# A decayed running sum by shifted additions on VectorE in place of products on TensorE

## The reference, cut to what matters

```
h      = rmsnorm(layernorm(x)) * g_res @ W_in.T + b_in
u      = rmsnorm(ctx)[:, :512] * g_init * exp(-0.001)
s[p]   = a * s[p-1] + u[p]            # the scan: a = 1 - exp(-0.001), about 0.001
x      = x + h + s[plug]
y      = layernorm(x); y_prev = y one row earlier
r      = sigmoid((mu_r*y + (1-mu_r)*y_prev) @ W_r)
k      = relu((mu_k*y + (1-mu_k)*y_prev) @ W_k) ** 2
out    = x + r * (k @ W_v)
```

## Time and profile before

| | us |
|---|---|
| median of 3 runs | 779.55 (778.33 to 780.54) |
| the profiled execution | 780.35 |
| its span | 778.8 |
| TensorE busy | 755.4 (97%) |
| VectorE busy | 556.2 (71%) |
| ScalarE busy | 413.7 (53%) |
| GpSimd busy | 175.5 (23%) |

### The profile page before, as it was taken

One profiled execution on the slowest core, in us unless ns is written; L12 is line 12 of the kernel. 1 busy time (PEld: TensorE's weight loads), 2 busy tenths in 40 slices (PEclk: granted clock), 3 DMA queues, 4 the chain that ended last, 5 costly groups with the idle time before them and its releaser, 6 DMA issues.

```text
span 778.8 us, 10909 instructions
## 1 busy us (share of the span) xinstructions
PE 755.4 (97%) x3462; PEld 621.9 (80%) x3463; DVE 556.2 (71%) x1005; ACT 413.7 (53%) x682; POOL 175.5 (23%) x175
## 2 busy tenths in 40 slices
PE   7878899999999999999999999999999999999997
PEld 4656688888888888888888888888888888888876
DVE  6797886766858677686776769577676967667552
ACT  4346565554546655455664545556454655544760
POOL 6622131313102131220313122131311213130000
PEclk9999999999999999999999999999999999999999
DMA  8556170524417053350705326071531706140011
GB/s 311 147 192 178 41 215 3 153 105 109 149 42 216 0 128 128 88 169 37 213 7 122 135 69 187 14 194 50 121 135 47 209 0 185 72 108 15 1 54 55
DMA packets 42765, 85.73 MB, mean 110 GB/s; under 512 B 3536, under 2 KB 3536, under 8 KB 42704
## 3 DMA queue, kind: packets, MB, share of 16 engines
q1 hardware_dynamic: 30768, 63.74, 21.8%
q0 software_dynamic: 9216, 16.78, 13.6%
q10 hardware_dynamic: 2736, 4.73, 1.8%
HBM read 64.26 MB, written 21.76 MB: 110 GB/s over the span
## 4 chain that ended last, share of the span: by engine, by line
PE 88%; DVE 4%; DMA 2%; issue 2%; ACT 2%; POOL 1%; SPq 0%; DVEq 0%; ACTq 0%; POOLq 0%
PE bank L494 28%; PE bank L495 28%; PE bank L496 28%; PE bank L599 3%; DMA xt<-in_x_turned 1%; POOL ring L433 1%; DMA s_rows<-scanned 1%; DMA ctx_rows<-in_ctx 1%; DVE ring L1034 1%; DVE xk_lo L908 1%; DVE scratch L1004 0%; DVE gate L1062 0%; ACT scratch L809 0%; DVE bn_a L937 0%; ACT scratch L807 0%
## 5 line engine op out<-in xcount | busy, mean ns | idle before, releaser
L433 POOL DMA_INDIRECT ring<-s_rows,patch_now x60 | 101.7, 1695 | 262.7 <-DMA s_rows<-scanned 231.0
L908 DVE TENSOR_TENSOR xr_lo<-scratch,xr_hi 128x512 fp32r<-128x512 f32 x124 | 85.6, 690 | 70.3 <-ACT xr_hi L715 69.8
L1004 DVE SCALAR_TENSOR_TENSOR scratch<-turned,cols,scratch 128x512 f32<-128x512 f32 x128 | 94.5, 749 | 31.5 <-ACT scratch L764 24.9
L715 ACT ACTIVATE turned<-bank 128x512 f32<-128x512 f32 x64 | 33.2, 604 | 137.1 <-PE bank L599 133.5
L494 PE MATMUL bank<-wi_hi,xt_hi 128*128 128x512 f32 x256 | 102.1, 399 | 3.3 <-DVE xt_lo L908 2.7
L494 PE MATMUL bank<-xk_hi,wk_hi 128*128 128x512 f32 x256 | 100.1, 391 | 3.4 <-DVE xk_lo L908 3.4
L494 PE MATMUL bank<-wr_hi,xr_hi 128*128 128x512 f32 x256 | 99.7, 390 | 1.0 <-DVE xr_lo L908 1.0
L495 PE MATMUL bank<-wi_lo,xt_hi 128*128 128x512 f32 x256 | 100.4, 392 | 0.0
L496 PE MATMUL bank<-wi_hi,xt_lo 128*128 128x512 f32 x256 | 100.2, 391 | 0.0
L496 PE MATMUL bank<-xk_hi,wk_lo 128*128 128x512 f32 x256 | 99.6, 389 | 0.0
L495 PE MATMUL bank<-xk_lo,wk_hi 128*128 128x512 f32 x256 | 99.6, 389 | 0.0
(11 more groups left out here) (134 smaller groups left out, 1283.4 us busy)
## 6 DMA issues: line engine op xcount, KB each, us to landing
ring<-in_x SPq DMA_DIRECT2D x16, 1024.0 KB, 7.4
out<-gate SPq DMA_DIRECT2D x64, 256.0 KB, 2.1
xt<-in_x_turned SPq DMA_DIRECT2D x14, 1024.0 KB, 5.2
ctx_rows<-in_ctx SPq DMA_DIRECT2D x16, 512.0 KB, 8.0
s_rows<-scanned ACTq DMA_DIRECT2D x16, 256.0 KB, 2.4
gate<-in_L_xattn_W_in SPq DMA_DIRECT2D x4, 256.0 KB, 6.2
xt<-in_x_turned SPq DMA_DIRECT2D x2, 512.0 KB, 8.0
ring<-in_x_turned SPq DMA_DIRECT2D x1, 1024.0 KB, 12.9
```

The source lines that it names most:

```text
L433: pool.indirect_dma_start(ring[b.slot][:, t, :], None, s_rows[:, :], bass.IndirectOffsetOnAxis(ap=rows, axis=0), compute_op=ALU.add).then_ ...
L715: return nc.scalar.activation(to, of, ACT.Copy)
L908: return nc.vector.tensor_tensor(to, whole, high, ALU.subtract)
L1004: nc.vector.scalar_tensor_tensor(scratch[:, 2 + i % 2, :], turned[:, c, 1:S + 1], cols[:, 1 + which, c:c + 1], scratch[:, i % 2, :], ALU.m ...
```

## The change

From the third batch on (new = 2 to 15), `scan_input` is followed by four steps on VectorE, with shifts k of 8, 4, 2 and 1 rows. For each, SP copies the current sum, moved down by k partitions, into a new tile `above`, in two DMAs within SBUF (112 rows, and the remaining 16 - k), and VectorE computes `scanned = above * a**k + (scanned or u)`. The first 8 rows of `above` are zeroed beforehand (`clear_head`). `add_bias` then adds the bias in SBUF. `u_high`, `u_low`, `scan` and `scan_out` are left out for these batches, and so are the waits of `turn` on the scan. `scan_input` moves ahead of the `ka_low`s, `add_out(b, 0)` and `add_out(b, 1)` ahead of the fourth step and of `far`. On SP the loads come in the order ctx, x, xt, followed by the copies of the four steps and the store of `scanned`, which leaves ScalarE's queue; the stores of the output come behind it. `far` splits its own `u` on VectorE (it isn't taken). New semaphores and the changes within `far` are cut from this diff.

```diff
@@ -69,6 +69,11 @@
             iteration(Batch(q, off))
     for n in range(rounds * RING + 1, count):
         iteration(Batch(0, n))
+def shift_steps(powers):
+    return [(k, powers[k] if k < len(powers) else 0.0) for k in (8, 4, 2, 1)]
 def decay_powers():
...
@@ -94,6 +99,9 @@
     SCAN = 3
     assert D == 512 and S == 512 and DG == 2 * D and B == 16 and H16 * W32 == S
     powers = decay_powers()
+    steps_of_scan = shift_steps(powers)
+    STEPS, MOST = len(steps_of_scan), P - 16
+    assert len(powers) <= 2 ** STEPS
     input_gain = math.exp(-EPSILON)
     with ExitStack() as stack:
...
@@ -322,22 +332,43 @@
             sp.wait_ge(w_lo_ready[WIN], C)
             load_w(WV, w_v)
+            def shift_scan(b):
+                since = b.plus(-2)
+                for n, (k, _) in enumerate(steps_of_scan):
+                    if n == 0:
+                        reached(sp, u_ready, b, 1, 1)
+                    else:
+                        reached(sp, earlier_added, since, STEPS, n)
+                    of = scanned if n else u
+                    sp.dma_start(above[k:k + MOST, :], of[0:MOST, :]).then_inc(earlier_loaded, 16)
+                    sp.dma_start(above[k + MOST:P, :], of[MOST:P - k, :]).then_inc(rest_loaded, 16)
+            def store_scan(b):
+                reached(sp, s_copied, b, 1, 1)
+                rows_added(sp, b.plus(-1))
+                sp.dma_start(s_rows[0:P, :], scanned[:, :]).then_inc(s_stored, 16)
             def iteration(b):
                 new = b.plus(2)
                 if new.exists(B) and not is_first(new, 1):
+                    reached(sp, far_over, new.plus(-1), 1, 1)
                     rows_added(sp, new.plus(-1))
-                    reached(sp, xt_lo_ready, new.plus(-1), 2, 2)
-                    load_xt(new)
+                    load_ctx(new)
                     reached(sp, out_ready, b.plus(-1), T, T)
                     if is_first(new, 2):
                         sp.wait_ge(w_lo_ready[WK], C)
                     load_x(new)
-                    reached(sp, far_over, new.plus(-1), 1, 1)
-                    load_ctx(new)
+                    reached(sp, xt_lo_ready, new.plus(-1), 2, 2)
+                    load_xt(new)
+                    shift_scan(new)
+                    store_scan(new)
                 if b.exists(B):
                     for t in range(T):
                         reached(sp, out_ready, b, T, t + 1)
...
@@ -592,9 +628,6 @@
                     reached(pe, yn_ready, b, T, t + 1)
                     if b.plus(-1).exists(B):
                         reached(pe, relu_ready, b.plus(-1), C, t + 1)
-                    if t == SCAN and b.plus(1).exists(B) and not is_first(b):
-                        reached(pe, s_copied, b.plus(1), 1, 1)
-                        reached(pe, far_over, b.plus(1), 1, 1)
                     for c in range(C):
                         last = nc.tensor.transpose(first_bank(b, t)[:, tile(c)], normed[:, t, c * P:(c + 1) * P],
                                                    ident[:, :])
...
@@ -623,7 +656,6 @@
                     for t in range(T):
                         value_product(b, t, 0, C)
                 if new.exists(B):
-                    scan(new)
                     far(new)
                 if b.exists(B) and not is_last(b):
                     for t in range(2, T):
...
@@ -842,7 +874,6 @@
                             squares_c(new)
                 if is_first(b):
                     squares(b)
-                    u_high(new)
                 if new.exists(B) and not is_first(new, 1):
                     x_hi(new, 0)
                     x_hi(new, 1)
...
@@ -857,10 +888,6 @@
                     u_high(new)
                     store_scan(new)
                     turned_out(nxt)
-                elif new.exists(B):
-                    if not is_first(b):
-                        u_high(new)
-                    store_scan(new)
                 if nxt.exists(B) and not is_last(nxt) and not is_first(nxt):
                     turned_out(nxt)
...
@@ -957,15 +984,52 @@
             def scan_input(b):
                 reached(dve, rs_c_done, b, 1, 1)
-                reached(dve, u_lo_ready, b.plus(-1), 1, 1)
+                if b.fixed and b.number() < 3:
+                    reached(dve, u_lo_ready, b.plus(-1), 1, 1)
+                else:
+                    reached(dve, earlier_added, b.plus(-3), STEPS, STEPS)
                 nc.vector.scalar_tensor_tensor(u[:, :], ctx_rows[:, 0:D], rs_c[:, :], g_ctx[:, :],
                                                ALU.mult, ALU.mult).then_inc(u_ready, 1)
+            def clear_head(b):
+                reached(dve, earlier_added, b.plus(-2), STEPS, 0)
+                nc.vector.memset(above[0:steps_of_scan[0][0], :], 0.0).then_inc(head_zeroed, 1)
+            def scan_step(b, n):
+                since = b.plus(-2)
+                reached(dve, earlier_loaded, since, 16 * STEPS, 16 * (n + 1))
+                reached(dve, rest_loaded, since, 16 * STEPS, 16 * (n + 1))
+                if n == 0:
+                    reached(dve, head_zeroed, since, 1, 1)
+                    reached(dve, s_stored, b, 16, 0)
+                    reached(dve, u_ready, b, 1, 1)
+                else:
+                    reached(dve, earlier_added, since, STEPS, n)
+                nc.vector.scalar_tensor_tensor(scanned[:, :], above[:, :], steps_of_scan[n][1], (scanned if n else u)[:, :],
+                                               ALU.mult, ALU.add).then_inc(earlier_added, 1)
+            def add_bias(b):
+                reached(dve, earlier_added, b.plus(-2), STEPS, STEPS)
+                nc.vector.tensor_tensor(scanned[:, :], scanned[:, :], bias[:, :], ALU.add).then_inc(s_copied, 1)
             def far(b):
                 n = far_count(dve, b)
                 with dve.If(n > 0):
                     earlier = far_earlier(dve, b)
+                    if b.fixed and b.number() < 2:
+                        reached(dve, s_done, b, 1, 1)
+                    nc.vector.tensor_copy(u_hi[:, :], u[:, :]).then_inc(far_u_hi, 1)
+                    dve.wait_ge(far_u_hi, earlier * T + 1)
+                    low(u_lo[:, :], u[:, :], f32(u_hi[:, :])).then_inc(far_u_lo, 1)
+                    dve.wait_ge(far_u_lo, earlier * T + 1)
                     for c in range(1, T):
                         done = earlier * (T - 1) + c
                         dve.wait_ge(far_loaded, done * 16)
...
@@ -1109,49 +1174,57 @@
                     ka_low(b, 2)
                     stats_a(new)
                     ka_low(b, 3)
-                    u_low(new)
+                    scan_step(new, 0)
                     norm_b(nxt)
                     gating(b, 0)
                     gating(b, 1)
+                    scan_step(new, 1)
                     x_lo(new, 0)
                     x_lo(new, 1)
-                    scan_out(new)
+                    scan_step(new, 2)
+                    add_out(b, 0)
+                    add_out(b, 1)
+                    scan_step(new, 3)
+                    add_bias(new)
                     far(new)
                     dve.sem_inc(far_over, 1)
-                    add_out(b, 0)
-                    add_out(b, 1)
                     gating(b, 2)
                     gating(b, 3)
                     add_out(b, 2)
                     add_out(b, 3)
                     return
                 if new.exists(B):
+                    clear_head(new)
                     stats_a(new)
                     stats_c(new)
                 if nxt.exists(B):
                     norm_b(nxt)
+                if new.exists(B):
+                    scan_input(new)
                 for m in range(C):
                     if b.exists(B):
                         ka_low(b, m)
                     if new.exists(B):
                         if m in (1, 2):
                             x_lo(new, m - 1)
-                        if m == 2:
-                            scan_input(new)
+                        if m in (2, 3):
+                            scan_step(new, m - 2)
                 if is_last(nxt):
                     mixing(nxt, 0, C)
-                if new.exists(B):
-                    u_low(new)
                 if b.exists(B):
                     gating(b, 0)
                     gating(b, 1)
                 if new.exists(B):
-                    scan_out(new)
+                    scan_step(new, 2)
+                if b.exists(B):
+                    add_out(b, 0)
+                    add_out(b, 1)
+                if new.exists(B):
+                    scan_step(new, 3)
+                    add_bias(new)
                     far(new)
                     dve.sem_inc(far_over, 1)
                 if b.exists(B):
-                    add_out(b, 0)
-                    add_out(b, 1)
                     gating(b, 2)
                     gating(b, 3)
                     add_out(b, 2)

```

(14 more changed lines are left out.)

## The result

The change makes the kernel slower: 785.36 us (780.35 to 791.42, 15 runs) against 779.86 (777.58 to 781.44, 15 runs), a ratio of 1.0073 with a 95% interval of 1.0059 to 1.0087. I had forecast 770.6 us, with 784 as the upper end of the range. The span of the profiled execution is 783.6 us.

The account below looks back on a forecast made before the run. TensorE's matmuls were taken to bound the kernel, narrowly even after the change: 780.35 - 9.5 for the scan matmuls + 0.6 at the entry = 771.4 us, or 770.6 as median; range to 8 in 10: 769 to 784.

Parts of the forecast that it names:

- L: Time from the end of one scan step to the next one's start, covering SP's wake and both copies: 2.3 us.
- the loop over xt: From xt's landing through ScalarE's copies, steps, store and gathers to the next xt: 45.1 us against TensorE's 45.3.
- rival 2: Transfers between steps slower, L above 2.6, so the kernel gets slower: 783.5 us at L = 2.7; chance 0.21, with rival 4.
- 38.2 + 3L: Length in us of the loop over xt per batch; said to exceed TensorE's period from L = 2.36.
- 38L - 98.6: Shift of the kernel's end in us for a given L, over 12 iterations and the entry, never below -9.5.
- The term of xt: In the loop over xt, from SP's first load to xt's landing, with ScalarE's wake: 9.3 us.
- those of the blocks and of the gathers: In the loop over xt: ScalarE's three relu, square and copy blocks 5.93 us; store's issue to SP's next load 15.6.
- The entry: Iteration 0, steps interleaved with other work: `scanned` of batch 2 ready at 98.2, third `ka_low` at 131.0; 0.6 us lost once.
- the 771.4: Forecast end in us for an execution like the profiled one, which is 0.8 above the median of the runs.
- rival 4: On VectorE, late gathers stall `add_x` and the mixing beyond TensorE's lead of some 4 us; counted within rival 2, at 0.03.
- The matmuls: Removing three scan matmuls saves TensorE 0.68 us a batch, 9.5 us in 14 batches; a batch then costs 45.29.
- VectorE's added work as work: About 2.7 us more per batch on VectorE, busy some 33 of 46 us, so hidden.

Follow-up runs that it names:

- first_copy: Changed kernel without the second copy (16 - k rows) of each step, so the last rows are wrong: 778.86 us, ratio 0.9969 to the kernel before.
- half_columns: Changed kernel with both copies of each step moving only 256 of the 512 columns: 779.11 us, ratio 0.9977 to the kernel before.
- xt_early: Changed kernel with the load of xt ahead of SP's wait for the gathers: 787.46 us, ratio 1.0109 to the kernel before.
- less_vector: Changed kernel with both layernorms' statistics over 128 of the 512 columns: 783.06 us, ratio 1.0055 to the kernel before.
- two_steps: Changed kernel with shifts of 2 and 1 rows only, bias in the third step's place: 770.18 us, ratio 0.9883 to the kernel before.
- no_copies: Changed kernel without the copies into `above`, zeroed once; the four steps run without waiting for transfers: 770.98 us, ratio 0.9880 to the kernel before.
- loads_only: Kernel before, scan still on TensorE, with the changed kernel's load order and the store of `scanned` on SP: 779.13 us, ratio 0.9984.
- three_steps: Changed kernel with shifts of 4, 2 and 1 rows, bias where it was: 770.12 us, ratio 0.9875 to the kernel before.

## Why the prediction was wrong

**What failed: the term L.** "The second copy has 8 to 15 rows, so 0.45 + 1.7 = 2.15 for it, 2.0 for the first, and with the wakes L = 2.3." The first copy takes 2.7, not 2.0, the second is issued 0.57 later and not 0.45, and L is 2.90. The nearest row was a store to DRAM of 256 KB, and I took its least value. first_copy shows that the large copy is most of it, half_columns that 0.5 us of it are the second half of its bytes. The mechanism was right: the loop over xt binds in each of the twelve trips. The sign is that of rival 2, to which I gave 0.21. Its point of decision, L = 2.6, was a little low: L of 2.67 and 2.71 still give no difference that matters, 2.90 is slower.

The formula of the Trainium skill ("DMA: Bandwidth & Descriptors", the anatomy of one DMA) spoke against the change, and was nearer than my row: an estimate of 2.5 us against 2.7 measured. But the page gives it for transfers issued from GpSimd, and these are issued from SP, which the prediction left out, so this is no test of it. For the half copy its estimate is 2.3 against 2.2, so the measured time grows twice as fast with the bytes. That the fixed part would be less for a target in SBUF, as I had read out of the page, the trace does not bear out: 2.7 for 224 KB within SBUF, 2.1 for 256 KB to DRAM.

**The other terms of the loop.** Over the twelve trips, with the forecast in brackets: from SP's first load to the start of `x_hi` 10.2 us (9.3); `x_hi` and the three blocks 7.5 (7.8); from there to the end of the first step 2.5 (2.5); the other steps and the bias 11.6 (9.84 at L = 2.3, 11.64 at 2.9); from the store to SP's next load 14.6 (15.6). The sum is 46.3. So the formula 38.2 + 3L, which gives 46.9 at L = 2.9, was 0.6 too long, and the loop falls under 45.3 at L = 2.56 and not at 2.36. L was off by 0.6, so this did not save the forecast; it is mainly why the kernel is 5.5 us slower and not the 11.6 of my formula 38L - 98.6. The term of xt was 0.9 too short, those of the blocks and of the gathers 0.4 and 1.0 too long; that they partly cancel is luck.

**The entry.** The changed kernel's `scanned` of batch 2 was ready at 98.15 as forecast (98.2), SP's load left at 114.67 instead of 113.2, xt landed at 124.5 instead of 122.5, and the third `ka_low` ended at 132.80 instead of 131.0, 1.8 us late. With this the forecast is accounted for: 12 x (46.3 - 45.29) = 12.1 us for the loop and 1.8 for the entry make 13.9, and from the 771.4 that I had for an execution like the profiled one to its 785.44 it is 14.0.

**A dip of the clock off the chain.** TensorE stood three times ahead of `value_product` of batch 1, 3.5 us together (its matmuls start at 129.32, 131.04 and 132.86). After that, its granted clock fell. The windows of the changed kernel (columns: busy time of PE, PEld, DVE, ACT, POOL, then the granted clock, the DMA share and GB/s):

```profile
120.00:132.80 12.80, 9.99 (x42) 7.22 (x40) 9.00 (x20) 7.94 (x13) 2.35 (x4) 0.96 0.34 126
...
132.90:138.30 5.40, 5.40 (x13) 4.24 (x14) 2.69 (x4) 0.95 (x2) 0.00 (x0) 0.50 0.15 47
...
138.60:143.00 4.40, 4.40 (x21) 3.62 (x20) 2.96 (x5) 0.00 (x0) 0.00 (x0) 1.00 0.19 59
```

For 5.4 us the granted clock is 0.50, the lower of the two levels, 1.2 GHz; a matmul then starts every 0.43 us instead of 0.23, which in 13 matmuls is 2.5 us. With the 3.5 this makes 6.0 of the 6.8 by which TensorE's first interval is too long. But the chain that ended last has no piece of TensorE there. In the next interval, 45.3 us, TensorE does not stand at all, though the loop's trip takes 47.8: it makes up there for what it lost. So by the chain the dip is not paid at the end. In half_columns, with less standing at this place, the clock between 120 and 145 us is 1.00 and the first interval 48.0. The runs of the changed kernel spread over 11 us and those of the kernel before over 4; the clock does not order them (780.35 us at a mean of 0.992, 786.14 at 0.996), and why they spread was not tested.

**The step that was missing: a second loop, through VectorE.** I had said that the gatings and `add_out`s between the steps, being shorter than L, cost nothing, and gave rival 4, VectorE itself, 0.03. Shorter than L is right, but VectorE cannot do anything else in what remains, 5.7 us in a batch. With these waits in it, the way from the gathers over `add_x` and VectorE's order to the steps and back takes 46.35 us in the trip of xt_early given above and 46.2 in the mean of its later intervals, as long as the loop over xt. In the changed kernel the chain that ended last does not go over it; xt_early, less_vector and the two together show that it takes over when the first is removed, and that both must go. So a better L would have helped both, a better order of the loads alone nothing.

**What was right.** The matmuls: the intervals of two_steps are 45.3, as 45.97 - 0.68. VectorE's added work as work (no_copies). The order of the loads and the store on SP (loads_only). The loop's course, which the chain of waits shows piece by piece, and its length to 0.6 us once L is known. That a few tenths of a us in one transfer decide.

**A version that beats both.** two_steps and three_steps take 770.2 and 770.1 us, 9 to 10 less than the kernel before, as much as the three matmuls are worth. a is about 0.001, so with the shifts 2 and 1 the first term left out is a to the fourth power, 1e-12 of the sum. Not tried: in the changed kernel the first step needs only `u` and a copy issued at 358.52, some 6 us before it starts at 364.42; only VectorE's order puts it behind the `x_lo`s. Ahead of the first of them (361.47) it could start 2.9 us earlier, an estimate, and the loop over xt would be shorter by as much.

## What to carry to other kernels

When work is moved off a full engine into a chain of transfers, add up every loop that closes over one batch, over all its trips and not over one, and count an in-order engine's waits as its work: here two loops of about 46.3 us stood against a bound of 45.3, and both had to come under it. A price that enters a loop three times should be measured before the change is built, or made irrelevant; here half of the steps carried nothing that float32 can hold. And what TensorE loses to stalls and to its clock is a loss of the kernel only where the chain that ended last goes through TensorE.

## What the runs showed of the hardware that I had not expected

A copy of 112 rows of 2 KB within SBUF lands in 2.7 us, later than a store of 128 such rows to DRAM (2.1 in the median of the changed kernel, 2.0 at the least), and one of 112 rows of 1 KB in 2.2. Its issue on SP takes 0.53 us, that of the copy of 8 to 15 rows 0.82, against 0.35 for the store of `scanned`. The granted clock fell to 0.50 for 5.4 us after 3.5 us of standing spread over 5 us. Instructions of VectorE had idle times of 2.8 us without a visible releaser behind the three jumps of the loop, and two of 3.0 in the written-out program, which has no jumps there.
